# Spline selection by predicated copies, a scatter through a spread array, and another order of the local attention's tick

## The reference

```python
# spline: each token has one of 64 tiles; a tile owns 4 of the 256 columns
u = clip((x_slice - mn) / (mx - mn + 1e-8), 0, 1 - 1e-6)      # 4 values a token
gi = clip(int(u * 16), 0, 15)                                 # cell of 16
b, s = spline_bases[tile, j, gi], spline_slopes[tile, j, gi]
delta = (b + s * (u * 16 - gi)) * output_scale[tile]
x = x + zeros.at[token, tok_dims].set(delta)
# local attention: 16 heads of 16, chunks of 64, each sees itself and the chunk before, band j in [i, i+64]
q, k, v = split(layernorm(x) @ w_qkv.T)
probs = softmax(where(band, q @ k.T / 4, -big))
x = x + (probs @ v) @ w_out.T
```

## Time and profile before

| what | value |
|---|---|
| time, median of 3 (lowest, highest) | 1135.63 us (1135.13, 1141.48) |
| profiled execution | 1140.07 us, of which span 1138.3 us |
| PE busy | 1029.1 us (90%) |
| DVE busy | 781.9 us (69%) |
| ACT busy | 711.1 us (62%) |
| POOL busy | 304.6 us (27%) |
| spline, first to last | 642.7 to 703.05 us of the span |
| local attention | 703.05 to 898.80 us of the span |

### The profile page before, as it was taken

One profiled execution on the slowest core, in us unless ns is written; L12 is line 12 of the kernel. 1 busy time (PEld: TensorE's weight loads), 2 busy tenths in 40 slices (PEclk: granted clock), 3 DMA queues, 4 the chain that ended last, 5 costly groups with the idle time before them and its releaser, 6 DMA issues. The chain is left out here.

```text
span 1138.3 us, 19082 instructions
## 1 busy us (share of the span) xinstructions
PE 1029.1 (90%) x6741; PEld 846.5 (74%) x6741; DVE 781.9 (69%) x1551; ACT 711.1 (62%) x1967; POOL 304.6 (27%) x249
## 2 busy tenths in 40 slices
PE   4999999999999999999687784799999799698997
PEld 3888888888888888899686663577775599574554
DVE  4897867667676767667467778867786444365775
ACT  4778766777767776767432372477776244556882
POOL 1352333323332323333101200244443100002442
PEclk9999999999999999999998957699999799799999
DMA  6211000000000010000340000000000000006432
GB/s 200 78 58 56 1 1 1 1 1 1 1 1 1 2 33 1 1 1 1 91 119 1 1 1 1 1 2 1 2 1 2 1 1 2 14 5 148 113 96 75
DMA packets 31981, 31.80 MB, mean 28 GB/s; under 512 B 8336, under 2 KB 23440, under 8 KB 31888
## 3 DMA queue, kind: packets, MB, share of 16 engines
q1 hardware_dynamic: 31888, 30.60, 9.8%
HBM read 28.36 MB, written 2.23 MB: 27 GB/s over the span
## 5 line engine op out<-in xcount | busy, mean ns | idle before, releaser
L329 POOL TENSOR_TENSOR roped_q<-roped_q,sin_q 128x512 f32<-128x512 f32 x64 | 82.0, 1281 | 315.6 <-DVE sin_q L466 315.6
L1580 ACT ACTIVATE win_P<-banks,win_neg_max 128x128 f32<-128x128 f32 x256 | 91.0, 379 | 40.2 <-DVE win_neg_max L1648 35.0
L406 ACT ACTIVATE oT_hi<-banks,bv_col 128x512 fp32r<-128x512 f32 x64 | 44.0, 688 | 87.5 <-PE banks L618 87.5
L329 POOL TENSOR_TENSOR roped_k<-roped_k,sin_k 128x512 f32<-128x512 f32 x64 | 84.0, 1313 | 46.3 <-DVE sin_k L466 46.3
L379 ACT ACTIVATE P<-banks,neg_max 128x128 f32<-128x128 f32 x256 | 90.2, 371 | 7.4 <-DVE neg_max L489 7.4
L1534 POOL TENSOR_TENSOR win_P<-win_P,win_inv 128x512 f32<-128x512 f32 x64 | 66.5, 1040 | 103.2 <-DVE win_inv L1653 103.0
L388 ACT ACTIVATE sin_k<-banks 64x512 f32<-64x512 f32 x128 | 75.9, 593 | 11.8 <-PE banks L37 10.3
L388 ACT ACTIVATE sin_q<-banks 64x512 f32<-64x512 f32 x128 | 75.9, 593 | 8.9 <-PE banks L37 6.6
L492 DVE SCALAR_TENSOR_TENSOR oT_lo<-banks,bv_col,oT_hi 128x512 fp32r<-128x512 f32 x64 | 48.0, 749 | 43.7 <-ACT oT_hi L406 43.1
L597 PE MATMUL banks<-WO_lo,oT_hi 128*128 128x256 f32 x256 | 73.7, 288 | 4.7 <-DVE oT_lo L492 4.7
L618 PE MATMUL banks<-PT,V 128*128 128x128 f32 x512 | 68.9, 278 | 6.6 <-ACT PT L402 6.5
(11 more groups left out here) (388 smaller groups left out, 3234.6 us busy)
## 6 DMA issues: line engine op xcount, KB each, us to landing
moe_gate_of<-moe_gate_rows SPq DMA_DIRECT2D x32, 256.0 KB, 3.9
X<-in_x SPq DMA_DIRECT2D x4, 512.0 KB, 5.7
stage<-in_wqT SPq DMA_DIRECT2D x4, 512.0 KB, 3.9
stage<-in_wvT SPq DMA_DIRECT2D x4, 512.0 KB, 5.6
stage<-in_woT SPq DMA_DIRECT2D x4, 512.0 KB, 3.9
ctx<-in_ctxT SPq DMA_DIRECT2D x4, 512.0 KB, 7.2
out<-X SPq DMA_DIRECT2D x8, 256.0 KB, 2.8
stage<-in_wkT SPq DMA_DIRECT2D x3, 512.0 KB, 3.9
```

The costliest lines, as they stand in the source:

```text
L329: nc.gpsimd.tensor_tensor(roped[w][:, p, :], roped[w][:, p, :], sin_part[w][:], ALU.add).then_inc(roped_sum[w], 1)
L1580: ins = nc.scalar.activation(P[:, h % 2, s, i, :], SC[2 * (h % 2) + s][:, i * 128:(i + 1) * 128], ACT.Exp, bias=neg_max[:, h % 2, at:at + ...
```

## The change

In the spline: `take_found` goes ahead of the residuals on ACT, and only four residuals stand between the halves; `normalise(3)` goes ahead of the wait for `cr_vo_hi`; three instead of four `project_ctx` stand ahead of L1441; the cell is chosen by four rounds of compare, subtract and a copy where the bit is set, each halving the cells that are left; `scatter` builds a spread array of 256 columns and adds it in one instruction; two instead of four batches are finished. In the local attention, the clearing of `win_V` moves from POOL to ACT, and 14 batches are left to finish, spread up to tick 15; each engine's tick has a new order.

```diff
-def scatter(nc, X, hot, delta, b):
-    for j in range(4):
-        columns = X[:, b, :].rearrange("p (t j) -> p t j", j=4)[:, :, j]
-        ins = nc.vector.scalar_tensor_tensor(columns, hot[:, b, :], delta[:, b, j:j + 1], columns, ALU.mult, ALU.add)
+def scatter(nc, dve, done, count, X, hot, delta, spread, some):
+    nc.vector.tensor_tensor(by_column(spread), hot[:, some, :]...broadcast_to([128, n, 64, 4]),
+                            delta[:, some, :]...broadcast_to([128, n, 64, 4]), ALU.mult).then_inc(done, 1)
+    dve.wait_ge(done, count)
+    return nc.vector.tensor_tensor(X[:, some, :], X[:, some, :], spread, ALU.add)
...
                     make_off(i)
+                    for p in range(4 * i, 4 * i + 4):
+                        take_found(p)
                     if i == 0:
-                        for b in range(HALF):
+                        for b in range(GROUP):
                             residual(b)
-                    for p in range(4 * i, 4 * i + 4):
-                        take_found(p)
...
                 normalise(2)
-                dve.wait_ge(vo_rounded, 1)
-                TT(flat(kept["cr_vo_lo"][:]), ...)
                 dve.wait_ge(rstd12_ready, 1)
                 normalise(3)
+                dve.wait_ge(vo_rounded, 1)
+                TT(flat(kept["cr_vo_lo"][:]), ...)
...
+                for k, m in enumerate((8, 4, 2, 1)):
+                    link(TS(bits[:, k], both, float(m), float(m), ALU.is_ge, ALU.mult))
+                    ins = TT(y[:], y[:], bits[:, k, :, 0, :], ALU.subtract)
+                    mask = bits[:, k]...broadcast_to([128, B, 2 * W, m])
+                    nc.vector.copy_predicated(left[:, :, :, 0:m], mask.bitcast(mybir.dt.int32), left[:, :, :, m:2 * m]).then_inc(chosen, 1)
+                    link(ins)
+                    dve.wait_ge(chosen, k + 1)
...
# local attention, ACT
                 for h in range(TICKS + 3):
-                    if p == 0 and 0 < m < PAIRS:
-                        take_v(m)
-                    if p > 0 and m + 1 < PAIRS:
-                        (round_xT, round_q, round_k)[p - 1](m + 1)
                     if 0 <= h - 1 < TICKS:
+                        exps(h - 1, 0)
                         exps(h - 1, 1)
+                    if m + 1 < PAIRS:
+                        (round_xT, round_q, round_k, take_v)[p](m + 1)
                     if p == 2 and m >= 1:
                         round_oT(m - 1)
-                    if h < TICKS:
-                        exps(h, 0)
# DVE (the order that this replaces is quoted above)
+                    take_PT(h - 2, 0)
+                    invert(h - 1, 0)
+                    invert(h - 1, 1)
+                    take_PT(h - 2, 1)
+                    if p < 3 and m + 1 < PAIRS:
+                        (split_xT, split_q, split_k)[p](m + 1)
+                    if p == 0: add_out(m - 2)
+                    find_max(h)
+                    if p == 2: split_oT(m - 1)
+                    if p == 1: restat(m - 2)
+                    if p == 2: normalise(m + 2)
+                    if h % 2 == 1 and h < 16: finish_batch(8 + h // 2)
# PE
+                    lay_band(h)
                     transpose_p(h - 2, 0)
-                    weigh(h - 3, 1)
                     if p == 0: project_out(m - 2)
                     (transpose_x, project_q, project_k, project_v)[p](m + 1)
                     transpose_p(h - 2, 1)
+                    score(h)
                     weigh(h - 2, 0)
+                    weigh(h - 2, 1)
```

More of the change, by code:

```diff
@@ L1110, in phase_spline @@
         y = sb("sp_y", [128, B, W])
[L1111 to L1114, removed]
+        bits = sb("sp_bits", [128, 4, B, 2, W])
+        frac = sb("sp_frac", [128, B, W])
         stat = sem("sp_stat")
@@ L1352, in _ @@
[L1352 to L1359, removed]
-                link(TT(coef[:, 2], coef[:, 2], coef[:, 0], ALU.add))
@@ L1363, in _ @@
+                link(TT(frac[:], y[:], left[:, :, W:2 * W, 0], ALU.mult))
+                link(TT(frac[:], frac[:], left[:, :, 0:W, 0], ALU.add))
+                link(TT(delta[:], frac[:], over(found[:, :, 128], W), ALU.mult))
                 dve.wait_ge(residual_ready, B)
-                for b in range(GROUP):
-                    scatter(nc, X, hot, delta, b).then_inc(scattered, 1)
-                for b in range(GROUP):
-                    dve.wait_ge(scattered, b + 1)
+                scatter(nc, dve, scattered, 1, X, hot, delta, wide[:, FIRST, :], FIRST).then_inc(scattered, 1)
@@ L1435, in _ @@
                         look_up(p)
-                for p in range(4):
+                for p in range(3):
                     project_ctx(p)
@@ L1446, in _ @@
                 ins.then_inc(ext_looked_up, 1)
-                for p in range(4, B // 2):
+                for p in range(3, B // 2):
                     project_ctx(p)
@@ L1466, in phase_window @@
         ident_b = sb("win_ident_b", [128, 128], BF16)
+        spread = sb("win_spread", [128, 2, D])
         xn = sb("win_xn", [128, 2, D])
@@ L1481, in phase_window @@
         inv = sb("win_inv", [128, 2, 8])
+        PARTS = slice(2, 4), slice(4, 8), slice(8, 12), slice(12, 16)
+        stat_done = [some.stop - DONE + 7 * (part + 1) for part, some in enumerate(PARTS)]
         consts_made = sem("win_consts_made")
@@ L1675, in _ @@
                 normalise(0)
+                finish_batch(2)
+                finish_batch(3)
+                split_xT(0)
+                finish_part(0)
                 finish_batch(4)
+                normalise(1)
                 finish_batch(5)
-                split_xT(0)
-                normalise(1)
+                split_q(0)
                 finish_batch(6)
-                finish_batch(7)
-                finish_norms(slice(DONE, HALF), 4, stat)
-                split_q(0)
-                finish_batch(8)
-                finish_batch(9)
                 split_k(0)
-                finish_batch(10)
                 for h in range(TICKS + 7):
                     m, p = h // 4, h % 4
-                    if 0 <= h - 1 < TICKS:
-                        invert(h - 1, 0)
-                    if 0 <= h - 3 < TICKS:
-                        take_PT(h - 3, 1)
-                    if p == 1 and m + 1 < PAIRS:
-                        split_xT(m + 1)
-                    if h < TICKS:
-                        find_max(h)
                     if 0 <= h - 2 < TICKS:
@@ L1775, in project_out, with lay_band @@
                     ins.then_inc(out_projected, 1)
+                def lay_band(h):
+                    wait(pe, exps_done, 2 * (h - 1))
+                    for s in range(2):
+                        nc.tensor.matmul(SC[2 * (h % 2) + s], ident_b[:], flat(band[:]), start=True, stop=True)
                 def score(h):
@@ L1781, in score @@
                         pe.wait_ge(k_lo_ready, 2 * i + 2)
-                    wait(pe, exps_done, 2 * (h - 1))
-                    for s in range(2):
-                        nc.tensor.matmul(SC[2 * (h % 2) + s], ident_b[:], flat(band[:]), start=True, stop=True)
                     for k in range(KD):
```

101 lines of the change are left out of this document (50 added, 51 removed).

## The result

| kernel | median of the runs (lowest, highest) | against the kernel before, with 95% interval |
|---|---|---|
| before, beside the changed kernel | 1136.68 us (1135.13, 1141.48) | |
| changed | 1165.76 us (1163.92, 1166.15) | 1.0245 [1.0223, 1.0266] |

The change costs 2.4%, 29 us on the medians. The profiled execution took 1166.15 us, of which the span is 1164.3. The windows of the changed kernel are cut at the same events as the earlier trace rows: the spline, the start of the local attention up to the first `find_max`, the ticks up to the last one, and the end. Columns as in the earlier trace rows: us, busy us and count of each engine, PEclk, DMA, GB/s.

The account below looks back on a forecast made before the run. PE was taken to bound the old ticks, DVE the spline, and a DVE-ACT ring the new ticks. Spline -11.4, start -4.1, ticks +13.9 and end -4.5 sum to -6.1 us: 1135.63 to 1129.5 us, range 1121 to 1147.

Parts of the forecast that it names:

- The step that failed: Ticks: PE, POOL and ACT stay 0.3 us or more ahead at full clock, so nothing hides the 4.87 us chain.
- the ring: Ticks: chain through DVE and ACT between `find_max` starts, 4.87 us a tick plus extras; a pair 23.05 us against 20.02.
- Rival 2: Ticks: PE's clock falls, 3.5 us each; one a pair gives 1154 us (12%), two to four falls 1139 us (10%).
- the main case: Whole kernel: shorter spline, start and end outweigh longer ticks, 6.1 us gained, 1129.5 us; chance 60%.
- Term 1: Spline: `normalise(3)` goes in front of DVE's 3.66 us wait for ACT; 1.3 us gained.
- Term 2: Spline: copies first make the last `sp_found` earlier; 2.6 us gained of a 3.81 us wait, about 1.2 left.
- Term 3: Spline: with three `project_ctx` in front instead of four, DVE's 1.55 us wait for PE goes; 1.5 us gained.
- Term 4: Spline: choosing the cell by four rounds removes 7.25 us and adds 4.4, copies 2.7 of it; 2.9 us gained.
- Term 5: Spline: scatter and statistics of two batches instead of four, 2.2 us against 5.3; 3.1 us gained.
- Start: Local attention up to the first `find_max`: clearing on ACT and fewer, shorter batches; 4.1 us gained of 16.69.
- End: After the last `find_max`: both weighings of tick 30 done early, 14.0 us against 18.51; 4.5 us gained.
- The spread of `finish_batch`: Ticks: it fits DVE's 2.9 us wait for exponentials, costing nothing up to tick 16; 9 us without that cover.

Follow-up runs that it names:

- the first experiment: Changed kernel with `round_oT` and `split_oT` moved to the front of their engines' tick with p = 2; 1143.28 us, ratio 1.0041.
- The fifth experiment: Changed kernel with the old tick order on PE, DVE and ACT, and the remaining batches finished in ticks 0 to 2 again; 1128.03 us, ratio 0.9913.
- the last experiment: Kernel before with the new tick order on PE, DVE and ACT and nothing else of the change; 1185.35 us, ratio 1.0422.
- second experiments: Changed kernel with the old tick order on PE, DVE and ACT, everything else of the change kept; 1118.11 us, ratio 0.9822.

## Why the prediction was wrong

It gave 1129.5 us and a range up to 1147; measured were 1165.8. By its own steps:

- **The step that failed** is the sentence in the ticks: "Does anything hide this? No: PE, POOL and ACT are ahead of the ring at each step by 0.3 us or more at full clock." In ticks with p = 2 PE is behind it. The chain was followed from `find_max` to `find_max` alone, and `split_oT`, which stands behind `find_max`, is in no term of the sum. But the first weighing of a pair waits for it, and so do the band, the transposes and the scores behind that weighing. Without that wait the ticks take 178.46 us and not 202.02, so this is 23.6 of the 27.5 us by which they missed.
- **The ring** was right: 5.46, 6.67, 4.88 and 6.07 us where 5.4, 6.7, 4.9 and 6.1 stood. With the wait away the 31 ticks are 4.0 us longer than the 174.5 computed; the middle pairs take up to 0.7 us more than 23.05.
- **Rival 2** named the fall of the clock, one a pair, at 3.5 us. Falls in the ring's gaps are real: the first experiment has seven of them without the wait, but its ticks are only 4.0 us over the sum, not 24.5. What made them dear is the wait: behind it PE is at the lower level for 3.4 us once and 6.8 us five times, just when the next scores are late. The rival priced the slow running alone and left out the late weighing itself (14.6 us over seven pairs with the gap filled), so it gave 1154 and not 1166. That it lies nearer to the measured time than the main case is in part luck.
- **Spline, -9.9 for -11.4 us.** Term 1 is as computed: `normalise(3)` is ahead and the wait for ACT is 2.21 us instead of 3.66 (1.45 gained for 1.3). Term 2: the wait for `sp_found` is 1.06 us, where 1.2 were expected (3.81 before, 2.75 gained). Term 3: no wait for PE is left at L1325 (1.55 gained). Term 4 is the sum's mis-sized term: the choice takes 682.28 to 689.58, 7.30 us for 8.05 before, a gain of 0.75 and not 2.9. The first and last predicated copy on DVE:

```profile
682.68 1.74 DVE L1350 COPY_PREDICATED sp_found<-sp_bits,sp_found 128x1024 f32<-128x1024 int32 x1
...
687.90 0.70 DVE L1350 COPY_PREDICATED sp_found<-sp_bits,sp_found 128x128 f32<-128x128 int32 x1
```

The four take 1.74 + 1.10 + 0.85 + 0.70 = 4.39 us against 2.7 estimated; the subtraction beside each is covered, the compare is not. Term 5: two instructions of 0.69 and statistics of 0.75 come to 2.2 with their gaps, as computed. Together 1.45 + 2.75 + 1.55 + 0.75 + 3.1 = 9.6 of the 9.9 us gained.

- **Start, -3.0 for -4.1 us.** The first two normalisations take 0.73 us as foreseen, but each `finish_batch` takes 1.25 us (0.41 + 0.42 + 0.43), not 1.17, and DVE waits 1.03 and 1.01 us for ACT (`win_k_hi`, `win_xT_hi`), 2.0 us where 0.8 were allowed for PE and ACT.
- **End, -3.0 for -4.5 us**; in the first experiment it is 13.7 us, for 14.0 predicted, at a clock of 1.00, so the order was read rightly. The changed kernel's end has a clock of 0.72; no run shows that this alone is the difference.
- **The spread of `finish_batch`** was taken as free of cost, and the 174.5 us hold no early stalls, while the 160.55 us of the old ticks do. The fifth experiment sizes the gain at 9.9 us in the old order. In the new order it is there too: the first four ticks take 28.4 us in the last experiment, which finishes the batches early, and 22.3 us in the changed kernel.

What stays open: how much of the 25 us between the first and second experiments is again clock (means of 0.92 and 1.00 in the ticks; the first one's pairs are up to 0.7 us longer than the ring), since no run had the ring at full clock throughout. And the first experiment's profile reaches the spline 2 us later than that of the changed kernel, ahead of any line that differs.

## What to carry to other kernels

When the order of in-order queues changes, follow every consumer of a buffer that is reused, not only the chain through the step that seems to set the pace: ask for each step that goes to the end of a tick which engine will stand for it, and what is queued behind that engine's wait. A step with slack for its own result may have none for the buffer that it frees. Put such steps into the time in which their engine waits anyway; the same rearrangement that lost 2.4% gains 2.3% when only the order on DVE and one step on ACT are different.

## What the runs showed of the hardware

- A predicated copy on DVE took 1.74, 1.10, 0.85 and 0.70 us for 1024, 512, 256 and 128 elements of 32 bits a partition, where a two-input operation of 1024 took 1.22 to 1.23. From these four, an estimate: some 0.6 us fixed and 1.1 ns an element. Short ones are dear.
- While PE stood for `split_oT`, 3.2 to 4.5 us, TensorE's clock fell to its lower level in five of six waits and 1.4 us behind the other; it came back 3.8 to 6.0 us after the five waits had ended. Sixteen matmuls without use in each of six such waits made the kernel 8.7 us faster.
- The clock also fell with no such wait: in the first experiment at about 760.0, 783.8 and 818.0, where the longest single gaps of PE just before were 1.0, 1.2 and 1.4 us.
